# Cross-attention head: scores and maxima in two stretches, and another split of the PSUM banks

## The reference

```python
q = _qdq(x) @ _qdq(wq).T + bq
kv = cond @ wkv.T + bkv
k, v = jnp.split(kv, 2, axis=-1)
attn = jax.nn.softmax(jnp.einsum('bnhd,bmhd->bhnm', q, k) * scale, axis=-1)
o = jnp.einsum('bhnm,bmhd->bnhd', attn, v).reshape(B, N, C)
out = _qdq(o) @ _qdq(wp).T + bp
```

## Time and profile before

| | us |
|---|---|
| median of 3 runs (665.68 to 669.96) | 666.28 |
| the profiled execution: its time | 667.73 |
| its span in the trace | 665.9 |
| TensorE (PE) busy, matmuls | 618.1 |
| VectorE (DVE) busy | 372.9 |
| ScalarE (ACT) busy | 298.4 |
| GpSimd (POOL) busy | 228.2 |

### The profile page before, as it was taken

One profiled execution on the slowest core, in us unless ns is written; L12 is line 12 of the kernel. 1 busy time (PEld: TensorE's weight loads), 2 busy tenths in 40 slices (PEclk: granted clock), 3 DMA queues, 4 the chain that ended last, 5 costly groups with the idle time before them and its releaser, 6 DMA issues.

```text
span 665.9 us, 12397 instructions
## 1 busy us (share of the span) xinstructions
PE 618.1 (93%) x4340; PEld 478.0 (72%) x4340; DVE 372.9 (56%) x680; ACT 298.4 (45%) x424; POOL 228.2 (34%) x120
## 2 busy tenths in 40 slices
PE   5999999999998999999999999998499899979998
PEld 3877788888885666666666666665289788769997
DVE  3796530332237777777777777754555333365552
ACT  3444233133324444444555555554236676744441
POOL 1000200000024777767777777771100544320000
PEclk9999999999999999999999999997689799979999
DMA  8673644443386555555555555520022224135520
GB/s 305 231 242 126 200 147 167 157 161 120 127 253 178 139 140 138 138 138 138 138 138 138 138 138 142 143 79 1 0 83 109 85 105 189 65 120 186 184 81 32
DMA packets 29757, 92.17 MB, mean 138 GB/s; under 512 B 5472, under 2 KB 9568, under 8 KB 23008
## 3 DMA queue, kind: packets, MB, share of 16 engines
q1 hardware_dynamic: 28480, 89.67, 44.5%
q10 hardware_dynamic: 1248, 2.10, 0.8%
HBM read 65.02 MB, written 18.35 MB: 125 GB/s over the span
## 4 chain that ended last, share of the span: by engine, by line
PE 83%; ACT 6%; DVE 5%; issue 3%; DMA 2%; POOL 1%; SPq 0%; ACTq 0%; POOLq 0%; DVEq 0%
PE ps L333 16%; PE ps L334 15%; PE ps L335 15%; PE ps L1254 10%; PE ps L1359 9%; PE ps L1347 8%; PE ps L1371 3%; ACT p_ring L689 3%; POOL p_sum L570 1%; PE ps L1333 1%; PE ps L1335 1%; DMA f_ring<-stream 1%; DMA k_stack<-kh_scratch 1%; PE ps L1496 1%; PE ps L1325 1%
## 5 line engine op out<-in xcount | busy, mean ns | idle before, releaser
L946 DVE TENSOR_REDUCE m_part<-ps 128x1 f32<-128x512 f32 (+1 forms) x256 | 165.5, 686 | 93.0 <-PE ps L1254 87.4
L689 ACT ACTIVATE p_ring<-ps 128x1024 f32<-128x1024 f32 x128 | 124.6, 1024 | 100.9 <-PE ps L1347 100.9
L570 POOL TENSOR_TENSOR p_sum<-p_sum,p_ring 128x1024 f32<-128x1024 f32 x60 | 142.8, 2380 | 11.6 <-ACT p_ring L689 7.5
L1254 PE MATMUL ps<-k_stack,q_max 96*128 96x512 f32 (+1 forms) x256 | 98.3, 438 | 3.6 <-DVE m_part L946 1.3
L1347 PEld LDWEIGHTS ps<-q_stack,k_stack 98*128 98x128 f32 x512 | 71.2, 191 | 18.6 <-ACT p_ring L689 11.0
L1347 PE MATMUL ps<-q_stack,k_stack 98*128 98x256 f32 x512 | 77.0, 289 | 7.8 <-ACT p_ring L689 7.8
L1359 PE MATMUL ps<-p_ring,v_head 128*32 128x256 f32 x1024 | 75.4, 390 | 0.1
L1254 PEld LDWEIGHTS ps<-k_stack,q_max 96*128 96x128 f32 x256 | 42.6, 188 | 42.7 <-issue 21.2
L333 PE MATMUL ps<-xt_h,h_ring 128*128 128x256 f32 x208 | 61.0, 293 | 2.2 <-DVE xt_l L1060 2.2
L334 PE MATMUL ps<-xt_l,h_ring 128*128 128x256 f32 x208 | 60.5, 291 | 0.0
L335 PE MATMUL ps<-xt_h,l_ring 128*128 128x256 f32 x208 | 60.4, 290 | 0.0
(11 more groups left out here) (183 smaller groups left out, 1016.6 us busy)
## 6 DMA issues: line engine op xcount, KB each, us to landing
f_ring<-stream SPq DMA_DIRECT2D x29, 1024.0 KB, 4.9
k_stack<-kh_scratch SPq DMA_DIRECT2D x60, 256.0 KB, 4.6
kh_scratch<-kh_buf SPq DMA_DIRECT2D x32, 256.0 KB, 5.5
kl_scratch<-kl_buf SPq DMA_DIRECT2D x32, 256.0 KB, 5.9
v_head<-v_all SPq DMA_DIRECT2D x16, 512.0 KB, 3.0
k_stack<-kl_scratch SPq DMA_DIRECT2D x30, 256.0 KB, 4.2
v_all<-stream SPq DMA_DIRECT2D x4, 256.0 KB, 4.7
f_ring<-stream SPq DMA_DIRECT2D x4, 256.0 KB, 5.7
```

Source lines behind the costliest of these rows:

```text
L570: nc.gpsimd.tensor_tensor(p_sum[:, p, :], p_ring[:, 0, :] if n == 0 else p_sum[:, p, :], p_ring[:, c % 4, :], ALU.add).then_inc(sums_done, 1)
L689: nc.scalar.activation(p_ring[:, c % 4, :], ps[:, 2 * (c % 2):2 * (c % 2) + 2, :].rearrange("p b n -> p (b n)"), ACT.Exp, scale=XSCALE).th ...
L946: nc.vector.reduce_max(m_part[:, mc0 + j // NT, j % NT:j % NT + 1], bank(4 + j % 2), AX.X).then_inc(max_read, 1)
L1254: nc.tensor.matmul(bank(to), q_max[p][0:SPLIT_ROWS, at128(j % NT)], k_stack[p][0:SPLIT_ROWS, k_at], start=True, stop=True).then_inc(max_do ...
```

## The change

The order of TensorE's program in a head is written anew. Two places show it, both in a head that is not in the loop (head 13). In these rows `q_max` belongs to maximum tiles, `q_stack` to score chunks (4 matmuls each), `v_head` to values (4 matmuls a chunk), `ones_col` to denominators, `pick` to the merge and `neg_hl` to the maximum rows.

Tiles of maxima now use three banks, and merges, maximum rows and outputs lie elsewhere. The core of the diff:

```diff
+        def maximum_bank(j):
+            return bank((6, 4, 6)[j] if j < 3 else 5 if j == 15 else 4 + j % 3)
...
-                nc.scalar.copy(o_t[:], bank(6)).then_inc(ot_evac, 1)
+                nc.scalar.copy(o_t[:], bank(7)).then_inc(ot_evac, 1)
...
-                    if c == 1 and not first:
+                    if c == 2 and not first:
                         evacuate_output(h - 1)
...
             def head(h, p, after=True):
                 first = isinstance(h, int) and h == 0
+                chunk_maxima(h + 1, 3, 15)
                 if not first:
                     normalize_output(h - 1)
+                chunk_maxima(h + 1, 15, 16)
+                negate_maximum(h + 1)
                 if not first:
                     output_maximum(h - 1)
+                if after:
+                    chunk_maxima(h + 2, 0, 2)
+                maximum_row(h + 1, 1 - p)
+                if after:
+                    chunk_maxima(h + 2, 2, 3)
...
+            def maxima(h, p, loads, first, last):
...
+                    if j == 0:
+                        pe.wait_ge(max_read, 16 * h - 1)
+                    elif j == 1:
+                        wait(pe, o_done, NT * (h - 2))
+                    elif j == 4:
+                        pe.wait_ge(mrow_ready, h)
+                    else:
+                        pe.wait_ge(max_read, 16 * h + (j - 1 if j in (2, 3, 15) else j - 2))
...
-            def merge(h):
+            def merge(h, last_two=False):
                 pe.wait_ge(ot_evac, h + 1)
+                if not last_two:
+                    pe.wait_ge(max_read, 16 * (h + 2) + 13)
...
-                if c == CHUNKS - 1:
-                    pe.wait_ge(sums_done, NSUMS * h + NSUMS)
-                    denominators(p_sum[:, p, :]).then_inc(sums_used, 1)
+            def summed_denominators(h, p):
+                pe.wait_ge(sums_done, NSUMS * h + NSUMS)
+                denominators(p_sum[:, p, :]).then_inc(sums_used, 1)
```

More of the change, by code:

```diff
@@ L1249, in project_queries, with first_maximum_tile @@
                         last.then_inc(q_done, 1)
-            def maximum_tile(j, to, k_at, p, before):
-                wait(pe, max_read, before - 1)
-                nc.tensor.matmul(bank(to), q_max[p][0:SPLIT_ROWS, at128(j % NT)], k_stack[p][0:SPLIT_ROWS, k_at],
-                                 start=True, stop=True).then_inc(max_done, 1)
-            def maximum_pass(h, p, loads, first, last):
+            def first_maximum_tile(j, k_at, read):
+                wait(pe, max_read, read)
+                nc.tensor.matmul(bank(4 + j % 2), q_max[0][0:SPLIT_ROWS, at128(j % NT)],
+                                 k_stack[0][0:SPLIT_ROWS, k_at], start=True, stop=True).then_inc(max_done, 1)
+            def maxima(h, p, loads, first, last):
                 for j in range(first, last):
@@ new lines, in score, with value @@
+                def score(c):
+                    scores(h, p, loads, c)
+                def value(c):
+                    values(h, p, loads, c)
+                next_maxima(3, 5)
+                score(0)
+                score(1)
+                next_maxima(5, 7)
+                if not first:
+                    summed_denominators(h - 1, 1 - p)
+                next_maxima(7, 8)
+                score(2)
+                next_maxima(8, 9)
+                score(3)
+                next_maxima(9, 11)
@@ new lines, in head @@
+                for c in range(3):
+                    value(c)
+                next_maxima(11, 13)
+                score(4)
+                next_maxima(13, 14)
+                score(5)
+                next_maxima(14, 15)
+                if not first:
+                    merge(h - 1)
+                score(6)
+                next_maxima(15, 16)
+                score(7)
+                if after_loads is not None:
+                    maxima(h + 2, p, after_loads, 0, 2)
+                for c in range(3, 7):
+                    value(c)
@@ L1391, in head, with last_head @@
+                maximum_rows(h + 1)
+                value(7)
+                if after_loads is not None:
+                    maxima(h + 2, p, after_loads, 2, 3)
+            def last_head(h, p, loads):
+                for i in range(4):
                     scores(h, p, loads, 2 * i)
                     scores(h, p, loads, 2 * i + 1)
-                    maxima(2)
-                    if i == 1 and not first:
-                        merge(h - 1)
-                    if i == 3 and next_loads is not None:
-                        maximum_rows(h + 1)
+                    if i == 0:
+                        summed_denominators(h - 1, 1 - p)
+                    if i == 2:
+                        merge(h - 1, last_two=True)
@@ L1400, in head @@
                         values(h, p, loads, 2 * i - 1)
-                    elif not first:
-                        values(h - 1, 1 - p, None, CHUNKS - 2)
-                        values(h - 1, 1 - p, None, CHUNKS - 1)
+                for c in (CHUNKS - 2, CHUNKS - 1):
+                    values(h, p, loads, c)
+                summed_denominators(h, p)
             maximum_rows(0)
             pe.wait_ge(ones_set, 3)
-            maximum_pass(1, 1, 1, 2, 4)
+            maxima(1, 1, 1, 2, 3)
             head(0, 0, 1, 1, 2, first=True)
```

73 lines of the change are left out of this document (30 added, 43 removed).

## The result

The changed kernel takes 640.5 us (median of 4 runs, 639.43 to 642.75), the kernel before 666.41 (median of 4, 665.68 to 669.96): a ratio of 0.9594, with a 95% interval of 0.9548 to 0.9639. 639 was forecast, with a range of 632 to 652. The profiled execution took 641.48, of which the span is 639.7; before it was 667.73 and 665.9.

The account below looks back on a forecast made before the run. TensorE's order was taken as the bound. Savings of 0.32 + 0.69 + 0.76 = 1.77 a head, taken as 1.73 from the built head, made 27.5 us with the ends: 639 us forecast, range 632 to 652.

Parts of the forecast that it names:

- That TensorE's order bounds the kernel: Whole kernel: TensorE, busy 618 of 665.9 us and holding 83% of the chain, sets the time by its order.
- Stretches, 0.32: TensorE's column-group stretches, four become three a head: one fewer saves 0.32 us, bounds 0.22 and 0.55.
- Three banks, 0.69: Maximum tiles with three banks: three pair waits of 0.23 a head go, saving 0.69 us, bounds 0.39 and 0.99.
- Copy later, 0.76: ScalarE's output copy behind chunk 1's exponential: score chunk 3's stall of 0.655 and restart of 0.105 go, 0.76 a head.
- What could be late next: Due times in the new head for keys, GpSimd's sums, merge, exponential 7, normalization: all hold, several by 0.1 to 0.3.
- It is covered by 0.2 only.: Keys of head h + 2, first half: landing at 10.2 us after tile 2 starts, tile 0 due at 10.4.
- rival of tight covers: At least five due times with 0.1 to 0.3 cover cost 0.5 to 0.9 a head: 646 to 652 us; chance 0.17.
- The chunk behind the merge: Score chunk 6 in the new head, priced like any other score chunk at 0.475 us.
- The ends: Heads 1 to 14 gain 14 x 1.73, head 0 1.7, head 15 1.6; its clock nothing, bounds -3 and +3.
- The bounds: Every bound at its low end, 1.37 a head, gives 644 us; at its high end 633.
- The signs: If right: maximum-row copies 14.5 apart, chunk 3 not waiting for ScalarE, three "issue" gaps of about 0.4 a head.
- first sign of being wrong: Gaps ahead of tile 0 of the head after next, ended by the key transfers, would show the forecast wrong.

Follow-up runs that it names:

- quarters: Changed kernel with the first half of a head's keys loaded in two quarters, the first already when score chunk 1 is done: 638.97 us, ratio 0.9555.
- best: Changed kernel with keys in quarters and maximum tile 15 directly behind the merge, ahead of score chunks 6 and 7: 639.77 us, ratio 0.9529.
- before_quarters: Kernel before with the first half of a head's keys loaded in two quarters, the first when score chunk 1 is done: 666.04 us, ratio 0.9944.

## Why the prediction was right

*That TensorE's order bounds the kernel.* Right. It held while the head shrank by 9%: no other engine became the bound.

*Stretches, 0.32.* Right. One stretch more costs 0.34, and entering, of which only bounds from 0 to 0.33 could be read before, is 0.10. The third stretch, of only eight matmuls, costs 0.10 to enter, 358.03 - 357.46 - 0.43 = 0.14 to leave, and 358.37 - 358.03 - 0.23 = 0.11 at the tile behind it, 0.35 in all. The Trainium skill (TensorEngine Tiling (Array Packing), Key Properties) says that a change of tiling mode drains TensorE; it gives no price and names no length, and the trace agrees with the prediction's reading of it, that a short stretch pays as a long one does.

*Three banks, 0.69.* The sum was near, its reading too narrow. Stretch and banks together gave 1.11 for 1.01, and that holds a fourth waiting pair of 0.24, which the late copy lays bare and the term had not counted. But taken out alone the third bank is worth 1.6, because the new order depends on it. 0.69 was read from the old order, and the price of one part of a change that leans on another cannot be read from before.

*Copy later, 0.76.* Right in the new order (0.77). In the order of before the same edit gives 0.15, and 0.54 when keys are no longer waited for. The exponential of chunk 1 ended 358.72 - 355.14 = 3.58 after tile 2 for 3.5, and chunk 3 started at 3.94 for 3.9.

*What could be late next.* GpSimd's sums, the merge, chunk 7's exponential and tile 10 held as worked out; no gap of theirs is in the head shown. The step that failed is the one on the keys of tile 0, "It is covered by 0.2 only." The landing was forecast 10.2 after the start of tile 2; it came 365.50 - 355.14 = 10.36 after it, and 0.26 passed from there to the weight load, where none had been counted. That and the restart cost 0.25 a head, which the run with quarters returned whole. Of the rival of tight covers this was the mildest form: one cover of the five gave way, by half of the least that rival asked for.

*The chunk behind the merge* was priced at 0.475 and is 0.56. No row of before had a score chunk there. Together with the keys this makes the head 14.88 instead of 14.54, and it is the whole difference. In the heads shown the gain is thus 16.27 - 14.88 = 1.39 for 1.73. Over the loop it is 1.52, because the heads of before took 16.42 on average: some of them waited for keys, which the prediction, reading one head of 16.27, had not seen.

*The ends.* Head 14 was counted at 1.73 and gave 14.90 - 14.28 = 0.62. Up to its mark it had four maximum tiles less than a loop head before, and two less now (16.27 - 14.90 = 1.37 and 14.68 - 14.28 = 0.40 against head 13), which the sum left out. Head 0 at full clock gave 15.25 - 13.38 = 1.9 for 1.7. The last head was counted at 1.6 and gave 1.4 for the value chunks, and 1.2 for the copy, which stalls chunk 3 there as elsewhere and was forgotten. The other 3.1 are the clock, counted at nothing with bounds of 3 either way, and came out at the edge of these bounds.

*The bounds.* Two of them do not come out of the working. The high ends add up to 0.55 + 0.99 + 0.76 = 2.30 a head, which gives 630 and not 633. And entering is taken at 0 in one term and at 0.33 in the other, at either end, though it has one price, 0.10.

*The signs.* Chunk 3 no longer waits, the copy stands where it was said, and the head shown has three gaps of 0.41 ahead of full-width stretches, two of them under VectorE's name. The copies are 14.90 apart and not 14.5, and the first sign of being wrong did appear, a gap ahead of tile 0 that the keys end.

So the total is better than its parts, and that is luck: about 5 us too much in the heads stand against 1.2 forgotten and 3.1 by the clock of the one execution that was profiled before. The medians hold some of that clock too. Among the runs on record with a mean granted clock of 0.979, the kernel before took 664.46, 664.51 and 664.87 and the changed kernel 641.32 and 639.77: some 24 us apart, on different chips, where 27.5 were forecast. The two profiles say the same: 26.2 less the 3.1, and 14.66 - 13.38 = 1.3 more for the low clock in head 0 of the changed kernel, is 24.4. The middle clock of the 47 runs of the kernel before that have one on record is 0.968, and that of ten of the changed kernel 0.976; how far the new order itself keeps the clock up was not tested.

## What to carry to other kernels

Price a reordering by distances between starts, build the new loop from them, and then list for each wait the time at which it is met: a cover of 0.2 us over a transfer of 4.6 was no cover, and a smaller first piece issued earlier cost nothing here and made all iterations alike. Edits in a loop with several nearly due waits do not add up: the same edit gave 0.15, 0.54 and 0.77 depending on what else was late, so test an edit both alone and with the next wait removed. When an order is made for a resource, the worth of that resource is to be measured in the new order and not in the old one.

## What the runs showed of the hardware

- From the landing of the keys to the first weight load that waits for them it is 0.23 to 0.27 us in the heads of the loop, and 0.06 outside it. The wait stands there with other waits against registers. Written out with constants it is 0.06 in ten of the twelve heads, but the first two groups of the merge then start 0.19 to 0.20 apart instead of 0.14.
- Behind the merge's eight small matmuls (widths of 32 and 1) a chunk of four matmuls takes 0.56 for 0.475, and a single tile 0.31 for 0.23. In best that tile's weight load starts at 360.60 and its matmul at 360.63, so nothing hides the load. By these two cases it costs about 0.08, whichever matmul comes first.
- The 1.2 GHz level came and went between executions of the same code: 6.9 us of the last head in the profile of before and none in that of before_quarters; part of head 0 in one profile of the changed kernel and none in the other (14.66 and 13.38); and head 0 of before_quarters, which has the order of before, took 223.96 - 205.52 = 18.44 us at a mean clock of 0.72, where that of before took 15.25 at 1.00. In the stretch ahead of the fall in the kernel before, TensorE had waited twice, for 0.95 and 0.96; in before_quarters the last head has the same waits and the clock stayed at 1.00.
- Three transfers of half of the keys, issued 0.4 to 0.5 apart, land 3.4, 4.2 and 4.7 us after their issue, at a DMA share of 0.60 in the head. The faster beat did not make them slower: over the twelve heads of the loop the third took 4.77 on average, and 4.78 before.
